# First pass of a four-layer kernel: exponentials of eight heads in two steps of four, and a new order of the pass

## The reference

```python
def _L0_xattn_ref(q, k, v, key_padding_mask, Wq, Wk, Wv, Wo, rel_emb):
    ...
    scores = jnp.einsum('bhqd,bhkd->bhqk', qh, kh) / math.sqrt(D_HEAD)
    ...
    scores = scores + bias.transpose(2, 0, 1)[None]
    scores = jnp.where(key_padding_mask, scores, -1000000000.0)
    attn = jax.nn.softmax(scores, axis=-1)
    out = jnp.einsum('bhqk,bhkd->bhqd', attn, vh)
    out = out.transpose(0, 2, 1, 3).reshape(Bq, Lq, D_MODEL)
    return out @ Wo.T

def _attn(x, ln_w, ln_b, conv_w, attn_w, proj_w, n_head):
    ...
    scores = jnp.einsum('bqhd,bkhd->bhqk', q, k) / jnp.sqrt(jnp.float32(D))
    ...
    p = jax.nn.softmax(scores, axis=-1)
    y = jnp.einsum('bhqk,bkhd->bqhd', p, v).reshape(B, T, C)
    return y @ proj_w

x = x + _L0_xattn_ref(_layernorm(x, axis=-1), ctx_1024, ctx_1024, ...)
x = x + _L0_ffn_ref(_layernorm(x, axis=-1), ...)      # _attn, then four routed experts
```

## Time and profile before

| | us |
|---|---|
| median of 3 runs | 2906.64 (2906.25 to 2918.45) |
| the profiled execution, its own time | 2907.73 |
| span in the trace, first to last instruction | 2905.9 |
| busy: PE / DVE / ACT / POOL | 2624.1 / 2450.1 / 2238.8 / 1369.0 |
| first pass | about 17 to 1062 |
| its even part, where all chains run | 89 to 1004, clock 1.00 |

### The profile page before, as it was taken

How to read it: one execution, slowest core, us unless ns; L and a number is a source line. 1 busy time by engine, 2 the same in 40 slices (tenths; PEclk the granted TensorE clock), 3 DMA queues, 4 the chain that set the end, 5 groups by cost and what they waited for, 6 DMA issues and landing times. The chain is left out here.

```text
span 2905.9 us, 77863 instructions
## 1 busy us (share of the span) xinstructions
PE 2624.1 (90%) x28466; PEld 1955.9 (67%) x28466; DVE 2450.1 (84%) x6675; ACT 2238.8 (77%) x5271; POOL 1369.0 (47%) x2097
## 2 busy tenths in 40 slices
PE   6999999999999858989999999798666999999998
PEld 4666666666666638986767776533265888888886
DVE  5899999999999834648999999579857999999995
ACT  3899999999999823436777777449748999999994
POOL 1344444444444413334555555100007888888884
PEclk8999999999999959989999999799987999999998
DMA  2012211111111002110111111000030000000000
GB/s 52 28 31 57 58 41 33 35 36 32 34 35 36 28 12 75 48 38 24 35 34 34 33 35 35 26 10 0 0 102 15 19 20 19 19 19 19 18 19 9
DMA packets 177545, 91.10 MB, mean 31 GB/s; under 512 B 46258, under 2 KB 173940, under 8 KB 177170
## 3 DMA queue, kind: packets, MB, share of 16 engines
q1 hardware_dynamic: 171634, 76.82, 9.9%
q0 software_dynamic: 4096, 8.40, 0.9%
q10 hardware_dynamic: 1440, 0.90, 0.1%
HBM read 43.71 MB, written 42.34 MB: 30 GB/s over the span
## 5 line engine op out<-in xcount | busy, mean ns | idle before, releaser
L2282 DVE TENSOR_TENSOR th<-tf,p_x 128x2048 f32<-128x2048 f32 (+1 forms) x192 | 470.0, 2450 | 5.8 <-ACT tf L2106 5.5
L2130 ACT ACTIVATE th<-th 128x2048 f32<-128x2048 f32 (+1 forms) x192 | 393.1, 2047 | 2.5 <-DVE th L2282 2.4
L2069 POOL TENSOR_TENSOR tl<-tf 128x1536 f32<-128x1536 f32 (+1 forms) x128 | 368.4, 2878 | 5.9 <-ACT tf L2106 5.9
L564 ACT ACTIVATE probf<-probf,colf 128x128 f32<-128x128 f32 x1024 | 313.2, 393 | 0.0
L2186 PE MATMUL p_rho<-th,late_w_row 128*32 128x128 f32 x6656 | 237.9, 279 | 0.0
L1674 PE MATMUL acc<-xnT_all,wT 128*128 128x512 f32 x384 | 181.3, 625 | 29.6 <-DVE tmax L1866 13.2
L454 POOL TENSOR_SCALAR col<-col 128x1 f32<-128x1 f32 x64 | 13.7, 214 | 391.0 <-DVE colc L889 342.4
L2138 ACT ACTIVATE tl<-tl 128x1536 f32<-128x1536 f32 (+1 forms) x128 | 196.1, 1532 | 0.0
L2186 PEld LDWEIGHTS p_rho<-th,late_w_row 128*32 128x32 f32 x6656 | 184.9, 110 | 14.0
L1096 POOL TENSOR_SCALAR col<-col 128x1 f32<-128x1 f32 x256 | 56.8, 222 | 268.8 <-DVE col L1385 191.8
L568 ACT COPY probTf<-fp 128x1024 f32<-128x1024 f32 x128 | 129.5, 1012 | 45.5 <-PE fp L712 45.5
(11 more groups left out here) (430 smaller groups left out, 8332.0 us busy)
## 6 DMA issues: line engine op xcount, KB each, us to landing
rows<-zeros SPq DMA_DIRECT2D x64, 256.0 KB, 2.4
cxT<-in_ctxT SPq DMA_DIRECT2D x128, 38.5 KB, 2.0
xb<-rows SPq DMA_DIRECT2D x67, 64.0 KB, 1.8
rows<-yb SPq DMA_DIRECT2D x67, 64.0 KB, 1.6
x<-in_x SPq DMA_DIRECT2D x64, 64.0 KB, 1.8
x_mid<-x SPq DMA_DIRECT2D x64, 64.0 KB, 1.5
z<-x_mid SPq DMA_DIRECT2D x64, 64.0 KB
x_next<-z SPq DMA_DIRECT2D x64, 64.0 KB, 1.5
```

The costliest lines, as they stand in the source:

```text
L564: last = nc.scalar.activation(scores, scores, ACT.Exp, bias=colf[s][:, 16 + HALF * hf + h:17 + HALF * hf + h])
L2069: nc.gpsimd.tensor_tensor(tl[i % NP][:, 0:shape[1], :], tf[s][:, POOLED[n]:POOLED[n + 1]].unsqueeze(2).to_broadcast(shape), tf[s][:, FEAT: ...
L2130: nc.scalar.activation(b, b, ACT.Tanh).then_inc(act_done, ACT_L.did(f"t{c}.tanh", e))
L2282: nc.vector.tensor_tensor(th[i % NT][:, 0:shape[1], :], tf[s][:, CHUNK[n]:CHUNK[n + 1]].unsqueeze(2).to_broadcast(shape), p_x[r][:, AT:AT ...
```

## The change

The step `f0a.exp` becomes `f0a.exp0` (heads 0 to 3) and `f0a.exp1` (heads 4 to 7), and `f0b.exp` likewise; f0a.PT and f0b.PT wait for `exp1`. `x0a.exp` becomes `x0a.exp0` and `x0a.exp` in the same manner. The instructions are the same, only that the list can put other steps between two halves, and that a semaphore is raised after each. All four tables of the first pass are new; of each table one line stands in the diff:

```diff
 PE_A = """
-    fc.rank@6 x0.o@2 f0.o@5 x0.T x0a.PT@1 f0a.S@3 x0.qkv fc.T@5 x0a.PV@1 f0a.PT@4 f0b.S@3 x0a.S x0b.PT@1 f0a.PV@4
+    x0a.PV@3 fc.T@7 x0a.S@2 f0a.PT@6 x0b.PT@3 f0b.S@5 f0a.PV@6 x0b.S@2 f0b.PT@6 x0b.PV@3 f0.T@4 fc.route@7 f0b.PV@6
...
 ACT_A = """
-    f0.yT@5 f0a.exp@4 f0.v@3 x0.xT x0a.PTc@1 fc.xT@5 x0.v x0b.exp@1 x0a.yg@1 f0a.PTc@4 f0b.exp@4 f0a.yg@4 x0b.PTc@1
+    x0a.exp0@2 x0a.exp@2 x0.yT@3 f0.yT@6 f0a.exp1@5 x0.xT@1 f0.v@4 x0b.exp@2 x0a.PTc@2 x0.v@1 f0b.exp0@5 fc.xT@6
+    x0a.yg@2 f0b.exp1@5 f0a.PTc@5 x0b.PTc@2 f0a.yg@5 f0a.exp0@4 f0b.PTc@5 f0.xT@3 x0b.yg@2 f0b.yg@5
...
 DVE_A = """
+    f0.conv0@3 x0.norm fc.first@6 x0.rden@2 fc.pick@6 f0.rden@5 x0.y@2 f0.y@5 x0b.less@1 f0.rope@3 fc.taken@6
...
 POOL_A = """
-    fc.eps@6 fc.rstd@6 fc.scatter@7 x0.kblk@1 fc.z@6 f0.eps@3 f0.rstd@3 x0.eps x0.rstd f0.kblk@3
+    x0.eps fc.scatter@8 x0.rstd f0.kblk@3 fc.eps@5 fc.rstd@5 fc.z@5 x0.kblk f0.eps@2 f0.rstd@2
...
                         for h in range(HALF):
                             scores = prob0[s][:, hf, h * KEYS:(h + 1) * KEYS]
                             last = nc.scalar.activation(scores, scores, ACT.Exp, bias=col0[s][:, 16 + HALF * hf + h:17 + HALF * hf + h])
+                            if h == GROUP - 1:
+                                last.then_inc(act_done, ACT_L.did(f"{p}.exp0", e))
+                                yield
                         last.then_inc(act_done, ACT_L.did(f"{p}.exp", e))
...
-                    for h in range(HALF):
-                        scores = probf[s][:, hf, h * TOK:(h + 1) * TOK]
-                        last = nc.scalar.activation(scores, scores, ACT.Exp, bias=colf[s][:, 16 + HALF * hf + h:17 + HALF * hf + h])
-                    last.then_inc(act_done, ACT_L.did(f"{p}.exp", e))
-                    yield
+                    for g in range(2):
+                        for h in range(g * GROUP, (g + 1) * GROUP):
+                            scores = probf[s][:, hf, h * TOK:(h + 1) * TOK]
+                            last = nc.scalar.activation(scores, scores, ACT.Exp, bias=colf[s][:, 16 + HALF * hf + h:17 + HALF * hf + h])
+                        last.then_inc(act_done, ACT_L.did(f"{p}.exp{g}", e))
+                        yield
...
-                    pe.wait_ge(act_done, ACT_L.value(f"{p}.exp", e))
+                    pe.wait_ge(act_done, ACT_L.value(f"{p}.exp1", e))
```

More of the change, by code:

```diff
@@ L106 @@
 PE_A = """
-    fc.rank@6 x0.o@2 f0.o@5 x0.T x0a.PT@1 f0a.S@3 x0.qkv fc.T@5 x0a.PV@1 f0a.PT@4 f0b.S@3 x0a.S x0b.PT@1 f0a.PV@4
-    x0b.S f0b.PT@4 x0b.PV@1 f0.T@2 fc.route@5 f0b.PV@4 x0.ygT@1 f0.ygT@4 f0.qkv@2 x0.yT@1 f0.yT@4
+    x0a.PV@3 fc.T@7 x0a.S@2 f0a.PT@6 x0b.PT@3 f0b.S@5 f0a.PV@6 x0b.S@2 f0b.PT@6 x0b.PV@3 f0.T@4 fc.route@7 f0b.PV@6
+    x0.ygT@3 f0.ygT@6 f0.qkv@4 x0.yT@3 f0.yT@6 x0.o@3 f0.o@6 fc.rank@7 x0.T@1 x0a.PT@2 x0.qkv@1 f0a.S@4
 """
 ACT_A = """
-    f0.yT@5 f0a.exp@4 f0.v@3 x0.xT x0a.PTc@1 fc.xT@5 x0.v x0b.exp@1 x0a.yg@1 f0a.PTc@4 f0b.exp@4 f0a.yg@4 x0b.PTc@1
-    f0b.PTc@4 f0.xT@2 x0b.yg@1 f0b.yg@4 x0a.exp x0.yT@1
+    x0a.exp0@2 x0a.exp@2 x0.yT@3 f0.yT@6 f0a.exp1@5 x0.xT@1 f0.v@4 x0b.exp@2 x0a.PTc@2 x0.v@1 f0b.exp0@5 fc.xT@6
+    x0a.yg@2 f0b.exp1@5 f0a.PTc@5 x0b.PTc@2 f0a.yg@5 f0a.exp0@4 f0b.PTc@5 f0.xT@3 x0b.yg@2 f0b.yg@5
 """
 DVE_A = """
[L115 to L118, removed]
+    x0a.max@1 f0b.add@4 x0.stats f0.norm@3 x0.aggr x0b.add@1 x0b.max@1 f0.conv2@3 fc.max@6 f0.conv1@3 fc.eq@6
+    f0.conv0@3 x0.norm fc.first@6 x0.rden@2 fc.pick@6 f0.rden@5 x0.y@2 f0.y@5 x0b.less@1 f0.rope@3 fc.taken@6
+    f0.qk@3 x0.x@2 f0.x@5 fc.slot@6 fc.stats@5 fc.aggr@5 f0b.max@4 f0.stats@2 x0.kT fc.slot_i@6 x0.qT fc.norm@5
+    f0.aggr@2 f0a.add@3 f0a.max@3 x0a.add f0.h@2
 """
 POOL_A = """
-    fc.eps@6 fc.rstd@6 fc.scatter@7 x0.kblk@1 fc.z@6 f0.eps@3 f0.rstd@3 x0.eps x0.rstd f0.kblk@3
+    x0.eps fc.scatter@8 x0.rstd f0.kblk@3 fc.eps@5 fc.rstd@5 fc.z@5 x0.kblk f0.eps@2 f0.rstd@2
 """
```

## The result

| | before | changed | ratio |
|---|---|---|---|
| median of 20 runs each, us | 2908.01 (2898.95 to 2918.45) | 2923.13 (2916.05 to 2939.03) | 1.005, 95% interval 1.0036 to 1.0064 |
| profiled execution; its span | 2907.73; 2905.9 | 2924.05; 2922.3 | |
| median lap of the even part | 15.31 | 15.62 | |
| x0.T of element 5 to that of element 63 (L621 and L625) | 88.9 to 977.8 | 86.0 to 994.5 | |

The ratio, here and in the experiments, is that of the means; the times given are medians. The change makes the kernel slower by 15 us. That is half of the 29 that were forecast, and inside the range. All of it lies in the first pass: from x0.T of element 5 to x0.T of element 63 it takes 908.5 instead of 888.8 us (+19.7), the ramp ahead of that is 2.9 shorter, and what comes after takes the same within 0.4. The sum, 16.4, is the difference of the two spans.

The account below looks back on a forecast made before the run. It took a circuit round TensorE, ScalarE and VectorE, 15.31 us per lap, as the bound; 12.99 + 2.35 + 0.43 = 15.77, +0.46 over 59.8 laps is +28, ramp and drain +1: 2936 us, range 2914 to 2952.

Parts of the forecast that it names:

- the ramp: First pass from 17 to 89 us: x0b.less adds 0.7 to each of five laps; with the drain, taken +1.
- The circuit of the kernel before: Chain of waits round TensorE, ScalarE and VectorE, closing once per lap, 15.31 us, with eight exponentials ahead of f0a.yg.
- Rival A: x0a.S alone costs nothing on TensorE: lap 14.92, 2884 us, faster; chance 0.07.
- Rival C: On GpSimd x0.kblk comes late for x0a.S: laps 15.95 to 16.1, 2950 us, slower still; chance 0.18.
- Rival B: No change: lone x0a.S and its neighbours cost about 0.3 less than summed, lap 15.4 to 15.5, 2915 us; chance 0.13.
- 15.7 to 15.9: Lap length in us named beforehand as a sign that the prediction is right.
- x0a.PT to f0b.PT: TensorE's stretch of the lap: 8.50 before, 8.15 without the stop, forecast 8.87 in the new order.
- f0.rden to x0.x: VectorE's stretch of the lap: 2.29 before, forecast 2.35 with x0b.less moved in and other steps moved out.
- +0.85 - 0.25 + 0.12 = +0.72: TensorE's new order per lap: x0a.S alone +0.85, cheaper changes of shape -0.25, dearer ones +0.12.
- The extra for row-tiled into column-tiled: TensorE's switch from f0a.S to x0a.PV and f0b.S to f0a.PV: taken at 0, bounds 0 and 0.07 each.
- x0b.less: VectorE step moved between f0.y and f0.rope, claimed to add its slot of 0.69 to f0.rden to x0.x.
- a parallel circuit only through f0.T: Second chain from x0a.PT through f0.T, f0.conv2 and x0.x: 15.68 per lap, slightly under the first's 15.77.

Follow-up runs that it names:

- e6: Changed kernel's split steps in new tables that keep f0b.S beside x0a.S and x0b.less behind the statistics; 2911.98 us, 0.9996 against the kernel before.
- e9: e6 with fc.z moved earlier on GpSimd and x0.stats later on VectorE; 2889.68 us, 0.9922 against the kernel before.
- e8: e6 with the two halves of f0a's and of f0b's exponentials next to each other again; 2944.59 us, 1.0111 against the kernel before.
- e1: Kernel before with the halves of x0's heads exchanged, so x0a.S uses the same row groups as f0b.S; 2932.05 us, ratio 1.0072.
- e7: e6 with the halves of x0's heads exchanged, so x0a.S and f0b.S share row groups; 2939.14 us, 1.0101 against the kernel before.
- e5: Changed kernel with x0b.less moved back behind fc.aggr on VectorE; 2967.85 us, 1.0198 against the kernel before.
- e3: Kernel before with the exponential steps split, both halves standing where the one step stood; 2911.82 us, ratio 0.9997.
- e4: Changed kernel with f0a's and f0b's exponential halves next to each other again; 2990.07 us, 1.0261 against the kernel before.

## Why the prediction was right, and where it was off

**The side and the mechanism: right.** The circuit of the kernel before was the one that set the lap: its sum, redone for a new order, gave the changed kernel's lap within 0.15, and 14.9 to 15.0 for e6 and e9, where the commonest lap is 14.92. The split frees f0b.PT (no idle time there; e8 brings it back), and the lone x0a.S costs more than that. Rival A is out: the pair's 1.06 is a sharing of the array (e1 and e7, where only the halves of x0 change places). Rival C is out: kblk had 0.70 of slack, above all because fc.eps took 0.22 here and not 0.68. Rival B had the direction: the neighbours did cost less than I summed, by half of what it asked. With 15.62 the lap lies outside the 15.7 to 15.9 that the prediction named as its sign of being right, about halfway between the forecast's 15.77 and B's 15.4 to 15.5; the time fell inside the range because the range took in B's middle.

**The size of the lap: 0.31, not 0.46.** By the terms of the sum, in the lap shown above:

| term | forecast | measured |
|---|---|---|
| x0a.PT to f0b.PT | 8.87 | 8.76 |
| f0b.PT to f0.rden | 4.12 | 4.09 |
| f0.rden to x0.x | 2.35 | 2.36 |
| x0.x to x0a.PT | 0.43 | 0.42 |
| lap | 15.77 | 15.63 |

The term that was mis-sized is the first, "+0.85 - 0.25 + 0.12 = +0.72": it is 8.76 - 8.15 = +0.61. Its large part holds: x0a.S alone 0.86 into f0a.PT, f0b.S alone 1.05. The 0.11 lie in the small neighbours. x0.qkv, x0a.PV and fc.T were to take 1.61 and take 1.56; x0b.PT and f0a.PV, taken at 1.60 as before, take 0.97 + 0.58 = 1.55; the rest is 0.01 to 0.03 apiece, f0a.PT's 0.03 being more and not less than forecast. Part of the first came out of the old trace wrongly. In the earlier trace rows's lap f0a.PT (522.64) starts 0.66 behind x0a.PV, with no idle time shown on TensorE, and I took that for the step's price. Timeline of TensorE's weight loads in the same lap, kernel before:

```profile
521.97 0.38 PEld L610 LDWEIGHTS xp<-probT,vaug 77*32 77x32 f32 x16 [0.17 <-issue]
522.61 0.86 PEld L712 LDWEIGHTS fp<-ident,probf 128*128 128x128 f32 x8 [0.26 <-ACT xncT L509]
```

f0a.PT's first weight load had waited for fc.xT, which the code has it do since fc.T uses the same buffer; in the changed kernel x0a.PV takes 0.58 (528.98 to 529.56), and in e6, with f0a.PT behind it as before, 0.58 as well (540.52 to 541.10). A wait of the weight load doesn't always appear as idle time of the matmuls.

**The extra for row-tiled into column-tiled, taken at nothing: right.** (Row-tiled are the score steps, whose matmuls each use 32 rows of the array; column-tiled is PV, whose matmuls each use 32 columns; the transposes use neither.) f0a.S and f0b.S take 1.05 into x0a.PV and f0a.PV (532.58 to 533.63), against 1.06 into a full-array step. The draining that the Trainium skill speaks of (TensorEngine Tiling (Array Packing), Key Properties) adds nothing here that tells the two switches apart; what it costs in both, no run shows. And the Trainium skill's "strict FIFO, no reordering" (TensorE: Matmul & The Clock Gate, Part 3: Packing small matmuls, The mechanism) is not what the traces show: in e6 x0a.S's matmuls again start (542.15) ahead of f0b.S's last two (542.65), though f0b.S stands first in the list.

**x0b.less: the sum right, but 0.69 is not its price.** The stretch came out at 2.36 against 2.35, since VectorE works through it without a stop. But e5 shows that without x0b.less it would be 2.25: TensorE's f0.qkv bounds it from the other side. The prediction saw a parallel circuit only through f0.T; that this did no harm to the sum is luck.

**The rest of the sum.** +0.31 over the 58 laps from element 5 to 63 is 18, and a few irregular laps (17.2 and 16.2, before one of 15.9) make it 19.7; the ramp, taken at +1, gave 2.9 back, inside its bounds. The ramp is no test of its terms (five laps of x0b.less for 0.7): its clock differed, 0.83 in the mean from 17 us to element 5 in the kernel before and 0.95 in the changed one. With 0.46 a lap and +1 the forecast was 29; 19.7 - 2.9 - 0.4 is 16.4. So about 8 of the 14 us by which the forecast was too high lie in the lap and 4 in the ramp.

**What it missed altogether** is the chain through the DMA queue, fc.z to x0.stats. It did no harm here, but it decides e6.

## What to carry to other kernels

Two small steps that run at the same time on one array each look cheap where they stand: before moving one away, price it from a place in the trace where it stands alone. The circuit that closes once per lap can be added up again for a new order, but each stretch wants a look at what runs beside it, since a term in another engine's shadow (x0b.less, 0.69 long, 0.11 of cost) gives little back when it is taken out, and a chain that had slack in the old order (fc.z, store, load, x0.stats) can take the gain. Look at the granted clock of the long laps too: in e5 it made 18 of 45 us. A change that bundles a good part and a bad one is worth taking apart: the split steps alone cost nothing, used together with the pair kept and the store in time they give 0.8%, and in the order they came with the kernel lost 0.5%.

## What the runs showed of the hardware

- Two row-tiled steps on the same row groups, one behind the other, take 1.71 where they take 1.06 and 0.85 alone: they overlap by 0.20 (e1, e7). On different row groups the pair takes 1.05 to 1.06.
- From a row-tiled step of these into a column-tiled or full-array one there is no difference: 1.05 and 1.06.
- From the end of GpSimd's x + h to the first use of the next load into that buffer: 4.65 where that use waited for the load, of it 1.55 from the issue of the store to that of the first load (e6; 2.00 in e9).
- Three more semaphore updates a lap on ScalarE cost nothing that shows (e3, 15.31 against 15.31).
- The granted clock can fall to 0.50 in single laps of an even part whose other laps run at 1.00 and have the same waits of TensorE: eleven of e5's laps, 1.62 longer each. In the profiled executions of the kernel before, the changed kernel, e1 and e4 it did not fall there.
